# Four projections of a pair in one slot by halves of the array's rows, every second spell without a slot

## The chip, the cores and the metric

One core of a Trainium2 chip runs the whole program. The metric is the time of one execution in device microseconds; every comparison is between executions of two programs on the same chip.

## The reference

A transformer block on x of 4 x 1024 x 256 with a context of 4 x 64 x 192, all in float32, 16 heads of 64:

```python
h = _ln(x, g1, be1);  x = _attn(h, h, Wq1, Wk1, Wv1, Wo1, bo1) + x          # self-attention, 1024 keys
h = _ln(x, g2, be2);  x = _attn(h, context, Wq2, Wk2, Wv2, Wo2, bo2) + x    # cross-attention, 64 keys
h = _ln(x, g3, be3);  y = h @ Wp + bp                                       # 256 -> 2 x 1024
a, gate = y[..., :1024], y[..., 1024:]
x = a * gelu(gate) @ W2 + b2 + x
# _attn: q, k, v = projections to 16 heads of 64; softmax(q k^T / 8) v; @ Wo + bo
```

The change lies in the first line, the self-attention: each head's 1024 x 1024 scores, their softmax and the product with the values.

## The kernel before

**Spells.** Self-attention runs in NC = 64 spells. Spell C handles one pair of heads (pair P = C // 2, 32 pairs over four batches of x) and one half of the queries (c = C % 2, 512 of 1024). In what follows n = C % 16 is a spell's place in its batch. A spell on TensorE has three parts:

- eight rounds (one for each 128 keys): `score` (L464) makes the scores of both heads, three products of split operands each (L477) and one that subtracts the maxima (L481). The two heads use the array's upper and lower 64 rows, form `64*128`, and write different PSUM banks. Beside them `first_score` (L442) makes the unsplit scores of the next spell, from which VectorE takes the maxima (`row_max`, L777);
- `attend` (L484): the values' products, eight pairs of float32 matmuls on the left and right 64 columns of the array, form `128*64`. In even spells from C = 2 `sum_two` (L510, form `128*32`) stands ahead of them;
- a slot, `whole_array(slot(C))` (L533, L294), form `128*128`: `turn_max` (L457) turns the 128 x 128 tile of the next spell's maxima with one transpose, then come two `project_qk` (L418), each six matmuls of 512 columns. At c = 0 they make the second half of pair P + 1's queries and keys, at c = 1 the first half of pair P + 2's. Some slots also hold the turning of normalised rows for the next batch ("ln": n = 12 and 13, in the last batch 12 alone), four products with Wo of the batch before ("out1": n = 1 and 2 from the second batch on) or eight projections of values ("v": C % 8 = 7, but the last).

**Order.** Each engine's program is written out in one fixed order. TensorE's is the loop at L641 to L655. ScalarE: eight exponentials of 128 x 1024, copies of key sums, `write_oT` (L1103), then `split_qk` of the slot (L1076, its copy from PSUM). VectorE: 16 `row_max`, `gather_max` (L783), a reciprocal of the sums (L802), then the slot's jobs: `make_shift` (L790), `split_qk` (L769), and for "ln" `turn_half` (L730). GpSimd: seven additions of exponentials a spell, one scaling of an output, every second spell the splitting of a pair's weights.

**Banks.** There are eight PSUM banks: S0a, S0b, S1a, S1b take the rounds' scores in turn; T0 and T1 take head 0's first scores, PV and PJ head 1's, each bank every second round. The values' products go to S0a (in the last spell to PV). In a slot the maxima go to T1, the projections to S1b and PJ, "ln" to PV and T0. `bank_free` makes TensorE wait for the last reader of a bank.

Of the kernel before, what the change touches and what calls it, by code (L numbers as in the profile page):

```python
# [7 lines left out]
F32 = mybir.dt.float32  # L8
# [13 lines left out]
    ctx_turned ctx_product wq2_turned keys2_product values2_product ln_turned qk_projected v_projected first_scored0 first_scored1  # L22
# [26 lines left out]
def block_kernel(nc, x, ctx, Wq1, Wk1, Wv1, Wo1, bo1, Wq2, Wk2, Wv2, Wo2, bo2, Wp, bp, W2, b2,  # L49
# [33 lines left out]
    with stack:  # L83
# [115 lines left out]

        keys2_dram = nc.dram_tensor("keys2_all", (PART, B, KT * INNER), F32, kind="Internal").ap()  # L200
# [85 lines left out]
        def passed(C, t, half, head):  # L286

            return 2 * TILES * C + 2 * (CHUNKS * t + half) + head + 1
# [34 lines left out]
        def _(e):  # L323
# [93 lines left out]

            def project_qk(P, u, bank="PJ"):  # L418
                kind, c = (1 if u < 2 else 0), u % 2
                need.wait_ge(s.wqk_split, 2 * (P + 1))  # L420
                normed((1, P // PAIRS * CHUNKS + c))
                bank_free(bank)
                for i, (w, h) in enumerate(TERMS):
                    for k in range(KT):
                        last = e.matmul(banks[bank], wqk[:, P % 2, w, kind, k, :],  # L425
                                        hT[:, h, k, c * BANK:(c + 1) * BANK],
                                        start=(i == k == 0), stop=(i == 2 and k == KT - 1))
                last.then_inc(s.qk_projected, 1)
                free[bank] = ((s.split_lo, qk_of[P, u]),)
# [54 lines left out]
            def attend(R):  # L484
# [4 lines left out]
                bank = "S0a" if C + 1 < NC else "PV"  # L489
# [43 lines left out]
            def whole_array(jobs):  # L533
                for job in jobs:
                    if job[0] == "qk":
                        project_qk(*job[1:])
                    elif job[0] == "v":
                        project_v(*job[1:])
                    elif job[0] == "max":
                        turn_max(*job[1:])  # L540
                    elif job[0] == "out1":
                        out1(*job[1:])
                    else:
                        turn_half(*job[1:])

# [93 lines left out]
            project_qk(1, 0, "S1a")  # L639
            project_qk(1, 2, "S1b")  # L640
            for C in range(NC):  # L641
                for jt in range(TILES):
                    for part in range(len(TERMS) + 1):
                        for head in range(2):
                            score(TILES * C + jt, part, head)
                    if C + 1 < NC:
                        for head in range(2):
                            first_score(*next_part(C + 1, jt), head)
# [6 lines left out]
                whole_array(slot(C))  # L655
# [27 lines left out]
        def _(e):  # L683
# [85 lines left out]
            def split_qk(P, u, bank="PJ"):  # L769
# [4 lines left out]
                e.scalar_tensor_tensor(lo, banks[bank], SCALE if kind == 0 else 1.0, hi.bitcast(F32),  # L774
# [37 lines left out]
            def whole_array(jobs):  # L812
                for job in jobs:
# [4 lines left out]
                    elif job[0] == "max":  # L818
                        make_shift(*job[1:])
# [96 lines left out]
            split_qk(1, 0, "S1a")  # L916
            split_qk(1, 2, "S1b")
            for C in range(NC):
                b, n = divmod(C, BC)
                if C + 1 < NC:  # L920
                    for i in range(TILES):
                        for head in range(2):
# [63 lines left out]
        def _(e):  # L986
# [89 lines left out]
            def split_qk(P, u, bank="PJ"):  # L1076
# [4 lines left out]
                e.activation(qk[P % 2][:, 2 * kind, c * BANK:(c + 1) * BANK], banks[bank], ACT.Copy,  # L1081
# [21 lines left out]
            def write_oT(C):  # L1103
# [7 lines left out]
                e.copy(oT[:, P % PRING, c * BANK:(c + 1) * BANK], banks["S0a" if C + 1 < NC else "PV"]).then_inc(s.oT_written, 1)  # L1111
# [97 lines left out]
            split_qk(1, 0, "S1a")  # L1209
            split_qk(1, 2, "S1b")  # L1210
# [350 lines left out]
```

## Time and profile before

| | us |
|---|---|
| median of three executions (2042.30 to 2042.63) | 2042.55 |
| the profiled execution's own time | 2042.06 |
| its span | 2040.3 |
| TensorE matmuls busy | 2028.6 (99%) |
| GpSimd, VectorE, ScalarE busy | 1416.4, 1385.3, 1159.7 |
| granted clock of TensorE, mean | 1.00 |

The 64 spells run from 63.9 us to about 1512 us of the span. A matmul's recorded duration is longer than the time it takes from its neighbours, since matmuls are pipelined; the distance between starts is what a matmul costs. In the views a float32 matmul has two records, one of the split (float32r) operands one.

### The profile page before, as it was taken

Reading aid. Unit: us, or ns where it says so; the run is one execution under the profiler, and the core shown is the slowest. Engines: PE = TensorE matmul, PEld = TensorE weight load, DVE = VectorE, ACT = ScalarE, POOL = GpSimd, SP = SyncE. Lnnn points to the kernel's source line nnn. Section 1 sums busy time; section 2 is a strip of 40 time slices with the busy share of each in tenths; the row PEclk is TensorE's granted clock in tenths of the full one; section 3 lists DMA queues with packets and bytes.
Section 4 is the critical chain, followed back from the end, with each engine's and each line's share of the span. In section 5 each row is a group of like instructions: output and inputs, shape, how many; then the busy total and the mean of one; then the engine's idle time right before and its main releaser. Section 6 shows DMA issues by size and latency. Waiting matters only on the chain.

```text
span 2040.3 us, 31825 instructions
## 1 busy us (share of the span) xinstructions
PE 2028.6 (99%) x12500; PEld 1387.7 (68%) x12500; DVE 1385.3 (68%) x2124; ACT 1159.7 (57%) x1851; POOL 1416.4 (69%) x745
## 2 busy tenths in 40 slices
PE   8999999999999999999999999999999999999999
PEld 7665665666565566665655666566558999888888
DVE  6477677666767785578678566757777898754453
ACT  5566577544557675255667544657665666533332
POOL 2699799975979998679799867979895576300000
PEclk9999999999999999999999999999999999999999
DMA  7300000001000000010000001000010530000100
GB/s 229 124 7 21 6 7 16 6 6 47 17 11 6 16 6 6 1 63 6 6 6 22 6 1 52 6 6 1 22 47 16 145 84 1 1 21 22 42 11 31
DMA packets 46566, 58.74 MB, mean 29 GB/s; under 512 B 5969, under 2 KB 40401, under 8 KB 45265
## 3 DMA queue, kind: packets, MB, share of 16 engines
q1 hardware_dynamic: 46416, 56.71, 8.9%
q8 instruction: 98, 1.61, 0.3%
q14 instruction: 52, 0.42, 0.1%
HBM read 38.88 MB, written 17.83 MB: 28 GB/s over the span
## 4 chain that ended last, share of the span: by engine, by line
PE 99%; ACT 1%; DVE 0%; DMA 0%; issue 0%; SPq 0%; ACTq 0%
PE score L494 22%; PE score L477 18%; PE score L603 9%; PE score L481 6%; PE score L425 5%; PE attn_project L617 4%; PE attn_project L589 4%; PE score L559 4%; PE attn_project L425 4%; PE first_score L451 4%; PE attn_project L528 3%; PE score L437 3%; PE score L528 2%; PE attn_project L451 2%; PE first_score L518 2%; PE attn_project L437 1%
## 5 line engine op out<-in xcount | busy, mean ns | idle before, releaser
L1316 POOL TENSOR_TENSOR acc<-acc,pT 128x1024 f32<-128x1024 f32 x384 | 914.6, 2382 | 55.4 <-POOL acc L1316 0.9
L1100 ACT ACTIVATE pT<-score 128x1024 f32<-128x1024 f32 x512 | 525.7, 1027 | 102.8 <-PE score L481 59.1
L477 PE MATMUL score<-qk 64*128 64x512 f32 x3072 | 456.2, 399 | 1.5 <-ACT oT L1111 0.9
L494 PE MATMUL score<-pT,vT 128*64 128x512 f32 x2016 | 446.5, 595 | 0.0
L780 DVE TENSOR_REDUCE nmax<-first_score 128x1 f32<-128x512 f32 x512 | 347.9, 679 | 3.5 <-PE first_score L451 1.4
L780 DVE TENSOR_REDUCE nmax<-attn_project 128x1 f32<-128x512 f32 x512 | 347.1, 678 | 0.0
L477 PEld LDWEIGHTS score<-qk 64*128 64x128 f32 x3072 | 257.1, 184 | 120.7 <-ACT pT L1100 67.9
L494 PEld LDWEIGHTS score<-pT,vT 128*64 128x64 f32 x2016 | 139.1, 137 | 289.4 <-issue 251.8
L1313 POOL TENSOR_TENSOR acc<-pT 128x1024 f32<-128x1024 f32 x64 | 154.0, 2406 | 150.3 <-ACT pT L1100 150.3
L802 DVE RECIPROCAL sums<-sums 128x512 f32<-128x512 f32 (+1 forms) x65 | 214.4, 3299 | 57.5 <-ACT sums L1125 56.9
L481 PE MATMUL score<-shift,pick 64*128 64x512 f32 x1024 | 205.5, 391 | 0.0
L451 PE MATMUL first_score<-qk 64*128 64x512 f32 x512 | 200.8, 392 | 0.0
L451 PE MATMUL attn_project<-qk 64*128 64x512 f32 x512 | 200.6, 392 | 0.0
L603 PE MATMUL score<-hT,wp 128*128 128x512 f32 x768 | 183.9, 395 | 0.0
L1111 ACT COPY oT<-score 128x512 f32<-128x512 f32 x63 | 37.0, 588 | 229.8 <-PE score L494 229.8
L603 PEld LDWEIGHTS score<-hT,wp 128*128 128x128 f32 x768 | 142.4, 188 | 32.1
L1303 POOL TENSOR_TENSOR xres<-xres,rows 128x1024 f32<-128x1024 f32 x8 | 19.2, 2399 | 204.1 <-DVE xn L711 204.1
L774 DVE SCALAR_TENSOR_TENSOR qk<-score,qk 128x512 fp32r<-128x512 f32 x67 | 46.1, 690 | 151.7 <-ACT qk L1081 151.7
L1125 ACT COPY sums<-first_score 32x512 f32<-32x512 f32 x248 | 143.1, 577 | 9.1 <-PE first_score L518 6.2
L795 DVE TENSOR_TENSOR shift<-first_score,mask 128x512 fp32r<-128x512 f32 x64 | 44.2, 691 | 119.6 <-PE first_score L461 119.6
L1327 POOL TENSOR_TENSOR probs<-probs,rsum 128x1024 f32<-128x1024 f32 x32 | 61.0, 1907 | 91.5 <-DVE rsum L837 91.5
L1081 ACT ACTIVATE qk<-score 128x512 fp32r<-128x512 f32 x67 | 40.0, 598 | 143.6 <-PE score L425 143.6
(160 smaller groups left out, 3056.1 us busy)
## 6 DMA issues: line engine op xcount, KB each, us to landing
xres<-x_middle SPq DMA_DIRECT2D x10, 512.0 KB, 3.7
xres<-in_x SPq DMA_DIRECT2D x4, 1024.0 KB, 7.6
raw_qk<-in_L_xattn_Wq SPq DMA_DIRECT2D x32, 128.0 KB, 2.2
raw_qk<-in_L_xattn_Wk SPq DMA_DIRECT2D x32, 128.0 KB, 2.4
raw_v<-in_L_xattn_Wv SPq DMA_DIRECT2D x8, 512.0 KB, 4.1
keys_all<-keys SPq DMA_DIRECT2D x1, 4096.0 KB, 12.1
values_all<-values SPq DMA_DIRECT2D x1, 4096.0 KB, 12.4
out_x<-xres SPq DMA_DIRECT2D x7, 512.0 KB, 2.9
```

Source lines behind the costliest of these rows:

```text
L425: last = e.matmul(banks[bank], wqk[:, P % 2, w, kind, k, :], hT[:, h, k, c * BANK:(c + 1) * BANK], start=(i == k == 0), stop=(i == 2 and k ...
L451: last = e.matmul(banks[bank], qk[P % 2][r, w, q0:q0 + PART], qk[P % 2][r, 2 + h, half * BANK:(half + 1) * BANK], start=(m == 0), stop=(m ...
L477: e.matmul(bank, qk[P % 2][r, 2 + h, keys], qk[P % 2][r, w, queries], start=(part == 0), stop=False)
L481: e.matmul(bank, pick[r, :], shift[r, :], start=False, stop=True).then_inc(s.scored, 1)
L494: last = e.matmul(banks[bank][head * DH:(head + 1) * DH, :], vT[:, v_slot(D, jt), c0:c0 + DH], pT[:, jt, head, :], start=(jt == 0), stop=( ...
L603: last = e.matmul(banks[bank], wp[q][:, w, k, which, o:o + PART], hT[:, h, k, (c % 2) * BANK:(c % 2 + 1) * BANK], start=(term == k == 0), ...
L780: e.tensor_reduce(nmax[:, head, t, half:half + 1], banks[PASS_BANKS[head][half]], AX.X, ALU.max, negate=True).then_inc(s.row_max, 1)
L802: e.reciprocal(sums[:, C % 2, part], sums[:, C % 2, part]).then_inc(s.sum_inverse, len(halves))
L1100: e.activation(pT[:, jt].rearrange("p h n -> p (h n)"), SC[R % 2][:, :], ACT.Exp).then_inc(s.exponential, 1)
L1125: last = e.copy(sums[r * DH // 2:(r + 1) * DH // 2, o, :], banks[bank][g * DH // 2:(g + 1) * DH // 2, :])
L1313: e.tensor_tensor(total, pT[:, jt - 1], pT[:, jt], ALU.add).then_inc(s.probs_added, 1)
L1316: e.tensor_tensor(total, total, pT[:, jt], ALU.add).then_inc(s.probs_added, 1)
```

## The change

- `slot(C)` has no projections at c = 0; at c = 1 it makes all four of pair P + 2. 25 even spells (all but n = 12, and n = 2 from the second batch on) and C = 61 have nothing in the slot; there the values' products go to PV instead of S0a.
- Where such a c = 1 slot holds nothing else (17 spells: n = 3, 5, 9, 11 of each batch and n = 1 of the first), `project_qk_rows` does it by halves of the array's rows, form `64*128`: each `project_qk` of six matmuls of 512 columns over 128 rows becomes two turns of twelve matmuls of 256 columns over 64 rows. In a turn the upper rows work on one half of the 512 columns and the lower rows on the other, in two different banks; in the second turn they change over, and the halves add up in PSUM. Four such jobs go to the bank pairs FS (T0 and T1), PX (PV and PJ), S1 and FS again, in the order: first turns of jobs 1 and 2, second turns of 1 and 2, then the same for 3 and 4.
- In the other 13 c = 1 slots with projections all four are whole-array jobs as before, behind the slot's other work.
- `turn_max` is two float32 matmuls of 128 columns on the left and right 64 columns of the array, after the third pair of the values' products; `make_shift` moves ahead of VectorE's reciprocal.
- In the spell after a slot by rows, the first round has no first scores; those of its place are put around the second round's scores, head 1 ahead of head 0.
- Before the loop pair 1 gets all four projections instead of two.

```diff
+        HALF = BANK // 2
+        across = {"S1": SC[1][:, HALF:HALF + BANK], "PX": PX[:, HALF:HALF + BANK], "FS": FS[:, HALF:HALF + BANK]}
+        both = {"S1": ("S1a", "S1b"), "PX": ("PV", "PJ"), "FS": ("T0", "T1")}
...
         def slot(C):
-            jobs = [("max", C + 1, "T1")] if C + 1 < NC else []
...
-            jobs += [(*job, through[i % len(through)]) for i, job in enumerate(between)]
-            after = P + 1 + c
-            if after < B * PAIRS:
-                jobs += [("qk", after, 1 - c, "S1b"), ("qk", after, 3 - c, "PJ")]
+            jobs = [(*job, through[i % len(through)]) for i, job in enumerate(between)]
+            if c and P + 2 < B * PAIRS:
+                qk_banks = ("S1a" if "T0" in through else "T0", "T1", "S1b", "PJ") if between else ("FS", "PX", "S1", "FS")
+                jobs += [("qk", P + 2, u, bank) for u, bank in zip((0, 2, 1, 3), qk_banks)]
             return jobs
+        def by_rows(C):
+            return C >= 0 and any(job[-1] in both for job in slot(C))
+        def heads_of(C, n):
+            return (1, 0) if n == 0 and by_rows(C - 2) else (0, 1)
+        def value_bank(C):
+            return "S0a" if slot(C) else "PV"
...
+            def project_qk_rows(P, u, pair, turn):
+                kind, c = (1 if u < 2 else 0), u % 2
+                need.wait_ge(s.wqk_split, 2 * (P + 1))
+                normed((1, P // PAIRS * CHUNKS + c))
+                if turn:
+                    need.wait_ge(s.half_projected, half_of[P, u])
+                else:
+                    bank_free(*both[pair])
+                for i, (w, h) in enumerate(TERMS):
+                    for k in range(KT):
+                        for g in range(2):
+                            r, part = slice(g * DH, (g + 1) * DH), (g + turn) % 2 * HALF
+                            last = e.matmul(across[pair][:, part:part + HALF], wqk[r, P % 2, w, kind, k, :],
+                                            hT[r, h, k, c * BANK + part:c * BANK + part + HALF],
+                                            start=(i == k == turn == 0), stop=(i == 2 and k == KT - 1 and turn == 1))
+                            if i == 2 and k == KT - 1 and not turn:
+                                last.then_inc(s.half_projected, 1)
+                if turn:
+                    last.then_inc(s.qk_projected, 1)
+                    for bank in both[pair]:
+                        free[bank] = ((s.split_lo, qk_of[P, u]),)
...
             def turn_max(C, bank):
-                e.transpose(banks[bank][:, 0:PART], maxima[:, :], ident[:, :]).then_inc(s.max_turned, 1)
+                for head in range(2):
+                    m = slice(head * DH, (head + 1) * DH)
+                    last = e.matmul(banks[bank][m, 0:PART], maxima[:, m], ident[:, :], start=True, stop=True)
+                last.then_inc(s.max_turned, 1)
...
+            def rounds(C):
+                late = by_rows(C - 1) and C + 1 < NC
+                for jt in range(TILES):
+                    R = TILES * C + jt
+                    if late and jt == 1:
+                        first_score(*next_part(C + 1, 0), 1)
+                        for part in range(len(TERMS)):
+                            for head in range(2):
+                                score(R, part, head)
+                        first_score(*next_part(C + 1, 0), 0)
+                        for head in (1, 0):
+                            score(R, len(TERMS), head)
...
-            project_qk(1, 0, "S1a")
-            project_qk(1, 2, "S1b")
+            for u, bank in zip((0, 2, 1, 3), ("S1a", "S1b", "PV", "PJ")):
+                project_qk(1, u, bank)
             for C in range(NC):
...
                 for jt in range(TILES):
                     attend(TILES * C + jt)
-                whole_array(slot(C))
+                    if jt == 2 and C + 1 < NC:
+                        turn_max(C + 1, "T1")
+                slot_products(C)
...
@@ VectorE
-                        for head in range(2):
+                        for head in heads_of(C + 1, i):
                             row_max(*next_part(C + 1, i), head)
                     gather_max(C + 1)
+                    make_shift(C + 1, "T1")
```

## Rows read from the trace of the kernel before

**Rows 1.** The page: the chain by engine; a group (busy us, mean ns).
```profile
PE 99%; ACT 1%; DVE 0%; DMA 0%; issue 0%; SPq 0%; ACTq 0%
...
L494 PE MATMUL score<-pT,vT 128*64 128x512 f32 x2016 | 446.5, 595 | 0.0
```

**Rows 2.** Timeline of TensorE, C = 30 and 31 (start, duration, x records).
```profile
742.97 7.09 PE L494 MATMUL score<-pT,vT 128*64 128x512 f32 x32
749.98 0.33 PE L461 MATMUL first_score<-ident,maxima 128*128 128x128 f32 x1
750.07 1.64 PE L425 MATMUL score<-hT,wqk 128*128 128x512 f32 x6
751.55 1.56 PE L425 MATMUL attn_project<-hT,wqk 128*128 128x512 f32 x6
753.04 0.96 PE L477 MATMUL score<-qk 64*128 64x512 f32 x6
...
762.58 2.80 PE L494 MATMUL score<-pT,vT 128*64 128x512 f32 x12
```

**Rows 3.** Timeline, all engines, C = 61 to 62.
```profile
1473.62 2.74 PE L494 MATMUL score<-pT,vT 128*64 128x512 f32 x12
...
1477.05 0.96 PE L477 MATMUL score<-qk 64*128 64x512 f32 x6 [0.42 <-ACT oT L1111]
```

**Rows 4.** Timeline of TensorE in cross-attention: 256 columns, whole array, float32r.
```profile
1753.89 1.12 PE L589 MATMUL attn_project<-valuesB_lo,turned 128*128 128x256 f32 x8
1754.84 1.12 PE L589 MATMUL attn_project<-valuesB,turned_lo 128*128 128x256 f32 x8
```

**Rows 5.** Timeline of the weight loads in a round of C = 31.
```profile
757.36 0.18 PEld L451 LDWEIGHTS first_score<-qk 64*128 64x128 f32 x1
757.37 0.18 PEld L451 LDWEIGHTS attn_project<-qk 64*128 64x128 f32 x1
```

**Rows 6.** Timeline of ScalarE and VectorE, C = 30 and 31.
```profile
751.75 0.60 ACT L1081 ACTIVATE qk<-score 128x512 fp32r<-128x512 f32 x1 [1.06 <-PE score L425]
752.38 0.69 DVE L774 SCALAR_TENSOR_TENSOR qk<-score,qk 128x512 fp32r<-128x512 f32 x1 [1.34 <-ACT qk L1081]
...
754.51 0.69 DVE L780 TENSOR_REDUCE nmax<-first_score 128x1 f32<-128x512 f32 x1
...
764.20 0.17 DVE L787 TENSOR_REDUCE maxima<-nmax 128x8 f32<-128x16 f32 x1
764.28 3.35 DVE L802 RECIPROCAL sums<-sums 128x512 f32<-128x512 f32 x1
```

**Rows 7.** Timeline, all engines, the slot of C = 28 (n = 12).
```profile
707.57 0.33 PE L461 MATMUL first_score<-ident,maxima 128*128 128x128 f32 x1
707.74 0.60 PE L337 MATMUL attn_project<-ident,xn 128*128 128x128 f32 x4
708.17 0.60 PE L337 MATMUL first_score<-ident,xn 128*128 128x128 f32 x4
...
711.50 0.69 DVE L741 TENSOR_TENSOR hT<-first_score,hT 128x512 fp32r<-128x512 f32 x1
...
712.53 0.39 PE L451 MATMUL first_score<-qk 64*128 64x512 f32 x1
```

**Rows 8.** Timeline, all engines, the slot of C = 29 (n = 13).
```profile
728.21 0.33 PE L461 MATMUL first_score<-ident,maxima 128*128 128x128 f32 x1
...
732.17 0.69 DVE L741 TENSOR_TENSOR hT<-first_score,hT 128x512 fp32r<-128x512 f32 x1
```

**Rows 9.** Timeline of GpSimd, C = 30 and 31.
```profile
737.72 0.65 POOL L1267 TENSOR_SCALAR wqk<-raw_qk 128x512 fp32r<-128x512 f32 x1
738.45 1.30 POOL L1269 TENSOR_TENSOR wqk<-raw_qk,wqk 128x512 fp32r<-128x512 f32 x1
...
760.30 1.29 POOL L1322 TENSOR_TENSOR oT<-oT,sums 128x512 f32<-128x512 f32 x1
...
764.08 12.47 POOL L1316 TENSOR_TENSOR acc<-acc,pT 128x1024 f32<-128x1024 f32 x5
```

More of the change, by code:

```diff
@@ L198, in block_kernel, with place @@
                  "S1b": SC[1][:, BANK:], "T0": FS[:, 0:BANK], "T1": FS[:, BANK:], "PV": PX[:, 0:BANK], "PJ": PX[:, BANK:]}
+        HALF = BANK // 2
+        across = {"S1": SC[1][:, HALF:HALF + BANK], "PX": PX[:, HALF:HALF + BANK], "FS": FS[:, HALF:HALF + BANK]}
+        both = {"S1": ("S1a", "S1b"), "PX": ("PV", "PJ"), "FS": ("T0", "T1")}
+        def place(bank):
+            return across[bank] if bank in both else banks[bank]
         keys2_dram = nc.dram_tensor("keys2_all", (PART, B, KT * INNER), F32, kind="Internal").ap()
@@ L308, in slot @@
             through = ("PV", "T0") if between and between[0][0] == "ln" else ("PV", "S0b", "S1a")
-            jobs += [(*job, through[i % len(through)]) for i, job in enumerate(between)]
-            after = P + 1 + c
-            if after < B * PAIRS:
-                jobs += [("qk", after, 1 - c, "S1b"), ("qk", after, 3 - c, "PJ")]
-            return jobs
+            jobs = [(*job, through[i % len(through)]) for i, job in enumerate(between)]
+            if c and P + 2 < B * PAIRS:
+                qk_banks = ("S1a" if "T0" in through else "T0", "T1", "S1b", "PJ") if between else ("FS", "PX", "S1", "FS")
+                jobs += [("qk", P + 2, u, bank) for u, bank in zip((0, 2, 1, 3), qk_banks)]
+            return jobs
+        def by_rows(C):
[4 more added lines that the diff above has]
+            return "S0a" if slot(C) else "PV"
+        half_of = {job[1:3]: 2 * (i + 1) for i, job in enumerate(
+            job for C in range(NC) for job in slot(C) if job[-1] in both)}
         def last_out1(i):
@@ L488, in attend @@
                 need.wait_ge(s.exponential, R + 1)
-                bank = "S0a" if C + 1 < NC else "PV"
+                bank = value_bank(C)
                 if jt == 0:
@@ L531, in out1, with slot_products @@
                 free[bank] = ((s.x1_added, TILES * b + t + 1),)
-            def whole_array(jobs):
-                for job in jobs:
+            def slot_products(C):
+                if by_rows(C):
+                    jobs = slot(C)
+                    for two in (jobs[0:2], jobs[2:4]):
+                        for turn in range(2):
+                            for job in two:
+                                project_qk_rows(*job[1:], turn)
+                    return
+                for job in slot(C):
                     if job[0] == "qk":
@@ L544, in whole_array @@
                         turn_half(*job[1:])
+            def rounds(C):
[10 more added lines that the diff above has]
+                            score(R, len(TERMS), head)
+                    else:
+                        for part in range(len(TERMS) + 1):
+                            for head in range(2):
+                                score(R, part, head)
+                    if C + 1 < NC and not (late and jt == 0):
+                        for head in range(2):
+                            first_score(*next_part(C + 1, jt), head)
             def score2(i):
@@ L638, in _ @@
             turn_max(0, "T1")
-            project_qk(1, 0, "S1a")
-            project_qk(1, 2, "S1b")
+            for u, bank in zip((0, 2, 1, 3), ("S1a", "S1b", "PV", "PJ")):
+                project_qk(1, u, bank)
             for C in range(NC):
-                for jt in range(TILES):
-                    for part in range(len(TERMS) + 1):
-                        for head in range(2):
[L645 to L648, printed above, removed]
+                rounds(C)
                 if C == NC - 1:
@@ L915, in _ @@
             make_shift(0, "T1")
-            split_qk(1, 0, "S1a")
-            split_qk(1, 2, "S1b")
+            for u, bank in zip((0, 2, 1, 3), ("S1a", "S1b", "PV", "PJ")):
+                split_qk(1, u, bank)
             for C in range(NC):
@@ L1080, in split_qk @@
                     need.wait_ge(s.scored, 4 * TILES * (P - 1))
-                e.activation(qk[P % 2][:, 2 * kind, c * BANK:(c + 1) * BANK], banks[bank], ACT.Copy,
+                e.activation(qk[P % 2][:, 2 * kind, c * BANK:(c + 1) * BANK], place(bank), ACT.Copy,
                              scale=SCALE if kind == 0 else 1.0).then_inc(s.split_hi, 1)
@@ L1110, in write_oT @@
                     need.wait_ge(s.out1_product, TILES * b + TPC * (c + 1))
-                e.copy(oT[:, P % PRING, c * BANK:(c + 1) * BANK], banks["S0a" if C + 1 < NC else "PV"]).then_inc(s.oT_written, 1)
+                e.copy(oT[:, P % PRING, c * BANK:(c + 1) * BANK], banks[value_bank(C)]).then_inc(s.oT_written, 1)
             def copy_sums(C, bank="PJ"):
@@ L1208, in _ @@
                     fetch_table(ACT.Exp, 1)
-            split_qk(1, 0, "S1a")
-            split_qk(1, 2, "S1b")
+            for u, bank in zip((0, 2, 1, 3), ("S1a", "S1b", "PV", "PJ")):
+                split_qk(1, u, bank)
             for C in range(NC):
```

12 lines of the change are left out of this document (4 added, 8 removed).

## The prediction

> **What bounds the kernel now.** The page first: TensorE is busy for 99% of the span, the granted clock is 1.00 of full speed (2.4 GHz) throughout, and the chain that ended last is 99% TensorE [rows 1]. The other engines are busy for 57% to 69%. So in the 64 spells only two things change the time: work added to or taken from TensorE's queue, and waits of TensorE that were not there. Then TensorE's timeline by spell, which is very regular. An odd spell (C = 31) starts its rounds at 753.04 and its values' products at 762.58, 9.54 us; eight pairs of values' products take 7.0 us (742.97 to 749.98, the way out included); then one transpose, twelve projection matmuls and back to scores at 753.04 [rows 2]. Even spells have 1.0 us more for the sums.
>
> **Prices on TensorE.** I take distances between starts, and where a merged row hides the last start, its end less one recorded duration.
> - Values' products: 12 records in 2.74 us, the last one's 0.59 [rows 1] off, leaves 2.15 us for five steps of two records, 0.43 each [rows 3]. So a record of 512 float32 columns costs 0.43 us, two column halves at once; a pair of matmuls is two such steps.
> - Way from them to the whole array: they end at 742.97 + 7.09 = 750.06, the last starts 0.59 earlier, at 749.47; the transpose starts at 749.98, 0.51 later, against 0.43 in the stream: 0.09 [rows 2]. The transpose itself costs 0.09 (749.98 to 750.07).
> - Projections: 12 matmuls from 750.07 to 753.04, 2.97 us. Six start in 1.48 (to 751.55), the other six take 1.49 with the way out. The last six have ended at 751.55 + 1.56 = 753.11 by record, each 0.40 long, so their last starts at 752.71, and their five steps are 0.232 each. From there to the scores it is 0.33, 0.10 over a step; the first six took 0.08 over six steps. Together a visit to `128*128` costs 0.18 us beside its work.
> - Projection of 256 columns: whole-array float32r matmuls of that width run eight in 0.95 (1753.89 to 1754.84), 0.12 each [rows 4]. By rows two run side by side: the 40 pairs of 512 columns in a spell's rounds take 9.54 us with the changes of form in it [rows 2], 0.24 at most, as much as one whole-array matmul of that width, and the two weight loads of a pair start 10 ns apart, 757.36 and 757.37 [rows 5]. So I take 0.12 a pair.
>
> **Part by part**, as additions to the total. The number of projections stays 128, so their matmul time cancels except where the form changes.
>
> (1) *The turning of the maxima.* Now two float32 matmuls of 128 columns beside each other: two steps of a quarter of 0.43, 0.215 us, in place of a transpose of 0.09, 63 times: +13.5 - 5.5 = +8. From below it can't be under the two quarter steps, as nothing beside it leaves TensorE idle; from above a full 0.43. I take the quarter: columns set the step. Its wait: the maxima are gathered at 764.20 + 0.17 = 764.37 [rows 6], 1.8 us behind the start of the values' products at 762.58; the third pair ends 2.6 us behind it. Margin 0.8 us, in even spells 1.8; the other five pairs of values' products stand behind this wait, and after them the slot.
>
> (2) *Visits to the whole array.* Without one are now the 25 even spells, the 17 by rows and C = 61: 43 visits. 41 times 0.18 = -7.4. The slots of C = 61 and 62 held the transpose alone, and 1.28 us lay between the last values' product and the scores; of that 0.42 was a wait for ScalarE's copy out of S0a [rows 3]. A direct way is 0.51, so these two save 0.75 each less the transpose counted in (1), -1.3; in C = 61 the values' products now wait for the maxima of PV, about +0.6. Sum -8.1.
>
> (3) *By rows.* 48 pairs of 0.12 are 5.76 us against 24 of 0.2325, 5.58: +0.18, 17 times: +3. Bounds: from below 0.107 a pair, a quarter of the step of 0.43 as in (1), which gives -7.5 instead of +3 in all; the upper one stands under rival B.
>
> (4) *The bank pair FS, used twice in a slot.* Job 4 may start when VectorE has read job 1. A turn is six pairs, and the first pair after a change of form costs 0.1 more: job 1 ends behind 18 pairs, at 2.26 us of the slot, and job 4 could start behind 30, at 3.70. The last matmul of a job is over 0.16 behind its step (1.12 less seven steps of 0.12 is a duration of 0.28 [rows 4]); 0.04 later the copy starts (751.55 + 0.16 against 751.75), VectorE 0.63 after it, for 0.69 [rows 2, 6]. 2.26 + 0.16 + 0.04 + 0.63 + 0.69 and 0.04 back to TensorE are 3.82; the restart costs 0.1 again: +0.22, 17 times: +3.7. Bounds 0 and 0.6. The copy is not late: the exponentials ended long before, and VectorE's reciprocal of 3.35 us, now behind `make_shift`, ends about 6.9 us after the start of the values' products (2.6 + 0.2 for the maxima, 0.1, 0.69, 3.3); the slot starts at 7.1. The waits of a second turn for its first have the other job's turn, 0.72, as cover. Behind the slot the last job's operands are split 1.47 us after the scores start, as now (754.51 against 753.04); the first score in T0 comes at 1.8, which is what the changed order is for. Nothing there.
>
> (5) *n = 12, "ln" alone, four times.* The transposes into T0 end, and the next round's first score wants T0. Today 2.8 us of projections lie between, and T0 is free at 711.50 + 0.69 = 712.19, before the first score at 712.53 [rows 7]. Now the turning starts at 707.57, ends near 708.65, rounds start there, and the first score would come at 709.7. ScalarE's copy of the values and its pass over PV come first as today, so VectorE's four steps behind them move 0.1 at most: T0 is free at 712.1. Wait 2.4, restart 0.1: +2.5 each, +10. The 2.8 us of projections leave this slot, and nearly all of it comes back as a wait. Bounds 0 and 2.8.
>
> (6) *n = 13, "ln" and four projections, three times.* The third projection (u = 1) reads the rows that the same slot has just turned. They are split at 732.17 + 0.69 = 732.86 [rows 8]. The turning starts at 728.21, eight transposes of 0.11 (four from 707.74 to 708.17 [rows 7]), two projections of 1.4: 732.0. Wait 0.9 each: +2.8. Before, only the halves of the rows that were ready were projected there.
>
> (7) *Start and the rest.* Two changes of form for `turn_max(0)`, +0.5; in C = 0 the values' products wait for PV, +0.35. Slots with "out1" and "v" keep their work. GpSimd: seven additions of 12.47/5 = 2.49 are 17.5 us, a scaling 1.3, every second spell 2.0 of weights [rows 9]: 39.6 us for two spells, against about 40.6 of TensorE's. The short spells (17.8) let it fall about 3 us behind, the long ones (22.8) give it back; an exponential waits for the addition one spell back, at least 6 us away. Nothing.
>
> Sum: +8.0 - 8.1 + 3.0 + 3.7 + 10.0 + 2.8 + 0.9 = +20.3. By this the profiled execution of 2042.06 becomes 2062.4; the median of the runs lies 0.5 above that execution, so I predict 2063 us, 1.0% slower.
>
> One rule would move (3). The Trainium skill, TensorEngine Tiling (Array Packing), Instruction Overhead, gives each matmul about 60 cycles on top. At full clock, by that page, a pair of 256 columns would be an estimated 0.13 instead of 0.12, and the sum about 8 us higher. The trace disagrees: its 0.12 a matmul at this width [rows 4] holds whatever comes on top.
>
> **Rivals.**
>
> *A, the waits are covered.* If (4) to (6) come to nothing, +3.8 is left: 2046.3. For it: TensorE waits for almost nothing now. Against: (5) is arithmetic from four VectorE steps in a row.
>
> *B, two loads and two matmuls in 0.12 us are too many.* A pair by rows is four instructions; the densest row here is a load and a matmul in 0.11 us, four transposes from 707.74 to 708.17 [rows 7]. If that is a limit on instructions, or if the loads of both row halves share it, a pair costs 0.22: 48 x 0.10 = 4.8 us a slot, 82 in 17 slots: 2145. Against it: the two loads 10 ns apart [rows 5]. A partial case (0.13 to 0.16 a pair) adds 8 to 33. The Trainium skill, TensorE: Matmul & The Clock Gate, LDWEIGHTS, has a load last by its columns and not its rows, so halving the rows saves nothing: an estimated 0.107 us each, and if two went one after another, 0.21 a pair.
>
> *C, faster: a change of form costs more than I read.* In C = 61 and 62 the slot took 1.28 us for one transpose [rows 3]. If everything beyond a bare step of 0.43 is the visit and its drain, it is worth 0.85, not the 0.27 of visit and transpose, at all 43 places: 25 us more saved, 2038. It decides from 0.75 a visit. Against it: half of that 1.28 is named as a wait for a copy, and in ordinary slots the starts leave only 0.18.
>
> *D, the half-long spells put GpSimd on the path.* Margin 1.0 us in 40; if it is used up, some 1 to 2 us in each of 17: 2080.
>
> **How the numbers follow.** Forecast 0.72, A 0.08, B with its partial cases 0.10, C 0.06, D 0.04. The forecast's own range is 2054 to 2074: (5) and (6) may halve, (4) double, a pair be 0.115 to 0.13. For 8 in 10 with something of A, D and the mild part of B: 2048 to 2082. Within 0.2% (4.1 us) can't be told from no change: faster 0.07 (C), same 0.06 (half of A, a little of C), slower 0.87.
>
> **What would show it.** Starts of the values' products: third to fourth pair 1.07 apart instead of 0.86. A slot without work: 0.5 us from the last values' product to the scores. A slot by rows: 6.6 us, steps of 0.12 a pair, one stop of 0.2 ahead of job 4. At n = 12 an idle TensorE of 2.4 us ahead of a first score, released by VectorE's hT; at n = 13 one of 0.9 ahead of a projection. Wrong if a pair's step isn't near 0.12, if the two "ln" slots show no idle time, or if the maxima's matmuls wait for VectorE.

## The result, and the profile after

| | before | after |
|---|---|---|
| median, us (4 executions each, same chip) | 2042.59 (2042.30 to 2042.66) | 2066.70 (2066.26 to 2067.17) |
| ratio, 95% interval | | 1.0118 (1.0101 to 1.0136) |
| profiled execution, us | 2042.06 | 2067.17 |
| its span, us | 2040.3 | 2065.4 |

The kernel became 1.2% slower: 24 us by the medians, 25.1 by the spans. Forecast was 2063, with 2048 to 2082 as the range.

The page of the kernel after, busy time by engine and the chain by engine, to be read against [rows 1]:

```profile
PE 2041.1 (99%) x13916; PEld 1431.0 (69%) x13916; DVE 1385.3 (67%) x2124; ACT 1159.6 (56%) x1851; POOL 1416.2 (69%) x745
...
PE 95%; DVE 2%; ACT 1%; DMA 1%; issue 0%; POOL 0%; SPq 0%; DVEq 0%; ACTq 0%
```

TensorE bounds it as before, but VectorE now holds 2% of the chain that was 99% TensorE. The waits of TensorE (waited for: us in total, times, longest) say where. For these three lines the kernel before has no counterpart at these places:

```profile
PE first_score L500 <- DVE hT L817: 9.7, 4, 2.4
...
PE score L474 <- DVE hT L817: 2.4, 3, 0.8
...
PE attn_project L547 <- DVE nmax L856: 0.7, 2, 0.4
```

They sum to 12.8 us, half of the loss. Two waits for ScalarE at C = 61 and 62, 0.9 us in all before (one is in [rows 3]), are gone. The other half is work and clock. I lined up the 64 spells of both traces by the starts of their first rounds' score, first values' product and last values' product. Change after minus before, us:

| part of a spell | places | each |
|---|---|---|
| ahead of the first spell (12 projections more, 2.79) | 1 | +2.98 |
| values' products | 63 | +0.22 |
| slot, now empty (12 projections gone), without C = 62 | 24 | -3.05 |
| slot by rows (12 projections more) | 17 | +3.00 |
| slot with "v" or "out1" (12 more) | 10 | +2.74 |
| slot with "out1", n = 2 (12 fewer) | 3 | -2.86 |
| slot n = 12 (12 fewer) | 4 | -2.90 |
| rounds behind it | 4 | +2.52, twice 1.5 on top |
| slot n = 13 (12 more) | 3 | +3.72 |
| rounds n = 14 | 3 | -0.29 |
| slot C = 61, 62 (only the transpose before, empty now) | 2 | -0.76 |
| wait for PV ahead of the values' products, C = 0 and 61 | 2 | +0.12, +0.43 |

All other rounds stay within 0.05. The last spell starts 24.05 us later than before.

**The turning.** TensorE's timeline of the kernel after, C = 2 (start, duration, records, [idle before]):

```profile
117.47 2.80 PE L547 MATMUL attn_project<-pT,vT 128*64 128x512 f32 x12
120.10 0.39 PE L513 MATMUL first_score<-ident,maxima 128*64 128x128 f32 x4
120.32 4.46 PE L547 MATMUL attn_project<-pT,vT 128*64 128x512 f32 x20
124.71 0.96 PE L530 MATMUL score<-qk 64*128 64x512 f32 x6
```

From 120.10 to 120.32 are the 0.22 us of the two turning matmuls, with no idle time before them. Then the twenty records end at 124.78, their last starts at 124.19, and the scores start at 124.71: 0.52 without a slot.

**A slot by rows.** Timeline of the kernel after, C = 1, all engines:

```profile
100.90 0.99 PE L457 MATMUL first_score<-hT,wqk 64*128 64x256 f32 x12
101.72 0.87 PE L457 MATMUL attn_project<-hT,wqk 64*128 64x256 f32 x12
102.43 0.87 PE L457 MATMUL first_score<-hT,wqk 64*128 64x256 f32 x12
103.14 0.87 PE L457 MATMUL attn_project<-hT,wqk 64*128 64x256 f32 x12
103.35 0.60 ACT L1156 ACTIVATE qk<-first_score 128x512 fp32r<-128x512 f32 x1 [1.74 <-PE first_score L457]
103.85 0.87 PE L457 MATMUL score<-hT,wqk 64*128 64x256 f32 x12
103.98 0.69 DVE L850 SCALAR_TENSOR_TENSOR qk<-first_score,qk 128x512 fp32r<-128x512 f32 x1 [6.56 <-ACT qk L1156]
104.72 0.97 PE L457 MATMUL first_score<-hT,wqk 64*128 64x256 f32 x12
105.53 0.87 PE L457 MATMUL score<-hT,wqk 64*128 64x256 f32 x12
...
106.95 0.86 PE L530 MATMUL score<-qk 64*128 64x512 f32 x6
```

A turn of six pairs takes 0.71 us (101.72 to 102.43). The first takes 0.82. The fifth, ahead of job 4, takes 0.87, since job 4 waits for VectorE to have read `first_score`: 103.98 + 0.69 = 104.67, and job 4 starts at 104.72. Its restart makes the sixth turn 0.81. From the start of the last values' product to the scores the slot took 6.57 us.

**n = 12.** Timeline of the kernel after, C = 28 to 29:

```profile
720.40 0.60 PE L362 MATMUL first_score<-ident,xn 128*128 128x128 f32 x4
720.93 0.96 PE L530 MATMUL score<-qk 64*128 64x512 f32 x6
721.42 0.82 DVE L812 TENSOR_SCALAR attn_project<-attn_project,cols 128x512 f32<-128x512 f32 x1 [1.73 <-ACT hT L1116]
722.27 0.69 DVE L817 TENSOR_TENSOR hT<-attn_project,hT 128x512 fp32r<-128x512 f32 x1
722.88 0.81 DVE L812 TENSOR_SCALAR first_score<-first_score,cols 128x512 f32<-128x512 f32 x1
723.72 0.69 DVE L817 TENSOR_TENSOR hT<-first_score,hT 128x512 fp32r<-128x512 f32 x1
724.56 0.47 PE L500 MATMUL first_score<-qk 64*128 64x512 f32 x1 [2.44 <-DVE hT L817]
```

VectorE's four steps fill 721.42 to 724.41, and the first score in T0 stands behind the last of them, where before 2.8 us of projections ran [rows 7].

**The clock.** Windows of the kernel after behind the four waits of n = 12, C = 13, 29, 45 and 61 (length, busy time and records of each engine, granted clock, DMA share, GB/s), each from the end of the wait or up to one microsecond behind it:

```profile
343.90:347.40 3.50, 3.50 (x20) 3.27 (x19) 2.56 (x4) 1.02 (x1) 3.36 (x3) 0.51 0.02 5
...
724.60:728.10 3.50, 3.50 (x30) 3.17 (x32) 3.03 (x6) 1.94 (x2) 3.36 (x2) 1.00 0.00 0
1105.10:1108.60 3.50, 3.50 (x21) 3.16 (x19) 2.34 (x5) 1.58 (x2) 3.36 (x3) 0.51 0.01 2
1485.40:1488.90 3.50, 3.50 (x30) 3.04 (x32) 3.02 (x6) 1.92 (x2) 0.95 (x1) 1.00 0.00 0
```

Behind two of the four, TensorE runs at half speed (0.51, the level of 1.2 GHz), with 20 records in 3.5 us where 30 pass at 1.00. Their rounds took 4.05 and 4.08 us more instead of 2.52. That is 3.1 us in all, and I had no term for it.

### The profile page after: what moved, and what is told of

It is laid out like the page before. It is cut to its first block, busy times and chain, and to the rows that moved or that the text cites. A ratio compares the mean times of both kernels' runs of the same rounds, so it can differ in the third digit from the quotient of the medians.

```text
span 2065.4 us, 34701 instructions
## 1 busy us (share of the span) xinstructions
PE 2041.1 (99%) x13916; PEld 1431.0 (69%) x13916; DVE 1385.3 (67%) x2124; ACT 1159.6 (56%) x1851; POOL 1416.2 (69%) x745
## 4 chain that ended last, share of the span: by engine, by line
PE 95%; DVE 2%; ACT 1%; DMA 1%; issue 0%; POOL 0%; SPq 0%; DVEq 0%; ACTq 0%
PE score L530 17%; PE score L547 13%; PE attn_project L547 9%; PE score L683 9%; PE score L534 6%; PE attn_project L697 4%; PE first_score L500 4%; PE score L639 4%; PE attn_project L669 4%; PE attn_project L581 3%; PE score L486 3%; PE first_score L457 3%; PE score L581 2%; PE first_score L571 2%; PE attn_project L486 1%; PE first_score L474 1%
## 5 line engine op out<-in xcount | busy, mean ns | idle before, releaser
L530 PEld LDWEIGHTS score<-qk 64*128 64x128 f32 x3072 | 262.0, 185 | 119.2 <-ACT pT L1175 64.3
L547 PE MATMUL score<-pT,vT 128*64 128x512 f32 x1184 | 268.5, 595 | 0.0
L547 PE MATMUL attn_project<-pT,vT 128*64 128x512 f32 x864 | 195.7, 595 | 0.7 <-DVE nmax L856 0.7
L547 PEld LDWEIGHTS score<-pT,vT 128*64 128x64 f32 x1184 | 80.4, 137 | 143.5 <-issue 126.8
L850 DVE SCALAR_TENSOR_TENSOR qk<-first_score,qk 128x512 fp32r<-128x512 f32 x57 | 39.4, 691 | 159.5 <-ACT qk L1156 159.2
L547 PEld LDWEIGHTS attn_project<-pT,vT 128*64 128x64 f32 x864 | 58.8, 137 | 115.4 <-issue 93.7
```

The costliest lines, as they stand in the source:

```text
L530: e.matmul(bank, qk[P % 2][r, 2 + h, keys], qk[P % 2][r, w, queries], start=(part == 0), stop=False)
L547: last = e.matmul(banks[bank][head * DH:(head + 1) * DH, :], vT[:, v_slot(D, jt), c0:c0 + DH], pT[:, jt, head, :], start=(jt == 0), stop=( ...
```

## Experiments

The theory: turning the maxima in float32, the two "ln" slots and the form by rows each cost what their places in the table above show. The rivals: the cost comes from the other parts, and would stay if one of these is undone. The kernel before was run again beside the experiments, with a median of 2042.89 us beside the first four (`turn_only` to `four_banks`) and of 2042.50 beside the last four; each ratio is to the median beside it. Differences to `after` are taken across these measurements, and `before` lay within 0.4 us in all of them.

**turn_only**: the kernel before, with the new turning alone.

```diff
-            jobs = [("max", C + 1, "T1")] if C + 1 < NC else []
+            jobs = []
...
-                e.transpose(banks[bank][:, 0:PART], maxima[:, :], ident[:, :]).then_inc(s.max_turned, 1)
+                for head in range(2):
+                    m = slice(head * DH, (head + 1) * DH)
+                    last = e.matmul(banks[bank][m, 0:PART], maxima[:, m], ident[:, :], start=True, stop=True)
+                last.then_inc(s.max_turned, 1)
...
                     attend(TILES * C + jt)
+                    if jt == 2 and C + 1 < NC:
+                        turn_max(C + 1, "T1")
...
                     gather_max(C + 1)
+                    make_shift(C + 1, "T1")
```

> The kernel before, with one part of the change alone: the maxima are turned by two float32 matmuls of 128 columns among the values' products, behind the third pair, and the shift is made then. Slots and projections as before. My theory: two steps of 0.107 us for a transpose of 0.09, 63 times, +8 us, so 2051; the values' products last 0.22 longer in every spell and TensorE waits for nothing new. Rival, the wait: if the maxima come later than the third pair, TensorE stands there for VectorE and it costs more than 10. Rival, hidden: no difference from 2042.6.

Measured: 2052.33 (2051.88 to 2053.73), ratio 1.0048 (1.0035 to 1.0062), span 2050.5: 9.4 us more than before by the medians, 10.2 by the spans. Timeline of TensorE in this kernel:

```profile
767.64 2.80 PE L497 MATMUL score<-pT,vT 128*64 128x512 f32 x12
770.26 0.39 PE L463 MATMUL first_score<-ident,maxima 128*64 128x128 f32 x4
770.48 4.46 PE L497 MATMUL score<-pT,vT 128*64 128x512 f32 x20
```

The same 0.22 in each of 63 spells. The transpose that left the slot gave back 0.05 to 0.07, 0.10 to 0.11 in the "ln" slots and nothing at C = 61 and 62; the rounds didn't move. The last spell starts 10.35 us later, 10.0 of it from the spells and 0.3 from the start. So this part alone is 40% of the loss, and a transpose in the stream of whole-array matmuls was cheaper than its 0.09 in the trace looked.

**ln_covered**: the kernel after, with the projections around "ln" as before (two at n = 11, two at n = 12), so that n = 12 has its 2.8 us of cover back and n = 13 keeps its four.

```diff
-            if c and P + 2 < B * PAIRS:
+            if n in (BC - 5, BC - 4):
+                jobs += [("qk", P + 1 + c, 1 - c, "S1b"), ("qk", P + 1 + c, 3 - c, "PJ")]
+            elif c and P + 2 < B * PAIRS:
```

> The changed kernel, with the two spells n = 11 and n = 12 as before the change: two whole-array projections in each slot, so that two of them stand behind the turning of the rows at n = 12 again. Theory: the four waits for T0 (2.4 us each) go, the pair of spells (11, 12) gets 2.8 us shorter in each batch, -11; and the two stretches of half clock right behind two of these waits go with them, 1.5 us each, -3: 2052.5, granted clock 1.00 throughout. Rival: the half clock has another cause and stays: 2055.5. Rival: the wait only moves to another bank or to a later spell: 2064 or more.

Measured: 2053.71 (2052.72 to 2053.81), ratio 1.0052 (1.0040 to 1.0065), span 2051.9: 13 us less than after. Of TensorE's waits `first_score <- DVE hT` is gone and the one of n = 13 is left. The waits, and TensorE's timeline at C = 28 to 29:

```profile
PE score L476 <- DVE hT L819: 2.4, 3, 0.8
```
```profile
717.91 0.96 PE L532 MATMUL score<-qk 64*128 64x512 f32 x6
718.95 0.39 PE L502 MATMUL first_score<-qk 64*128 64x512 f32 x1
```

The first score follows the scores without idle time, and the granted clock is 1.00 in the windows where it had been 0.51. The wait at n = 12 and the clock behind it are worth 10.1 + 3.1; the experiment gives 13.0 by the medians, 13.5 by the spans. Its edit does more than take the wait away: the n = 11 slots lose their form by rows with the stop, and slots n = 11 and 12 together are 0.26 shorter, 1.0 us in all. The first spell starts 1.5 us later than in `after`, with nothing edited ahead of it. So the sum isn't exact to a microsecond. The wait and the half clock go at once; that the clock falls because of the wait rests on this and on its place, in every trace, at such a wait.

**turn_one_pass**: the kernel after, with the maxima and the identity in bfloat16, so that each turning matmul is one record. The maxima that are subtracted are thereby rounded to bfloat16.

```diff
-            ("maxima", [PART], F32),
+            ("maxima", [2 * PART], BF16),
...
-                    last = e.matmul(banks[bank][m, 0:PART], maxima[:, m], ident[:, :], start=True, stop=True)
+                    last = e.matmul(banks[bank][m, 0:PART], maxima[:, m], ident_h[:, :], start=True, stop=True)
...
+            e.tensor_scalar(ident_h[:, :], ident[:, :], 1.0, 1.0, ALU.mult, ALU.mult).then_inc(s.const, 1)
```

> The changed kernel, with the maxima and the identity in bfloat16 for the turning, so that the two matmuls of 128 columns are one record each instead of two float32 records. The shift of a row is rounded, the same for the whole row. Theory: columns set the price, so a quarter of the float32 price: 0.055 instead of 0.215 us a spell, -10 us, 2056.6. Rival: a matmul that short has a floor of its own, such as the transpose's 0.09 to 0.11: -7, 2060. Rival: what the turning costs is the two entries and their loads, not the columns: no change, 2066.7.

Measured: 2059.60 (2059.02 to 2059.67), ratio 1.0082 (1.0068 to 1.0096), span 2057.8. By the medians it gives 7.1, between the two expectations, and needs both traces to be read. Timeline of TensorE, C = 2:

```profile
117.96 2.80 PE L549 MATMUL attn_project<-pT,vT 128*64 128x512 f32 x12
120.59 0.23 PE L515 MATMUL first_score<-ident_h,maxima 128*64 128x128 bf16 x2
120.64 3.60 PE L549 MATMUL attn_project<-pT,vT 128*64 128x512 f32 x16
```

The turning takes 0.05 to 0.06 now, so all of the 0.16 a spell came, 10.1 us, and the rival's floor of 0.09 to 0.11 isn't there. But half clock stood behind all four "ln" waits in this profile, not two. Its windows at C = 13 and 61:

```profile
342.00:346.00 4.00, 3.98 (x21) 3.66 (x23) 2.50 (x4) 1.02 (x1) 3.86 (x2) 0.57 0.00 0
...
1479.00:1483.00 4.00, 4.00 (x25) 3.77 (x24) 2.90 (x6) 2.05 (x2) 2.38 (x1) 0.59 0.00 0
```

Two more times 1.5 us take 3 of the 10 back.

**four_banks**: the kernel after, with a bank pair for each job of a slot by rows, so that no job waits for VectorE; the first scores of the next spell go head 0 first, as FS is read first.

```diff
-        across = {"S1": SC[1][:, HALF:HALF + BANK], "PX": PX[:, HALF:HALF + BANK], "FS": FS[:, HALF:HALF + BANK]}
-        both = {"S1": ("S1a", "S1b"), "PX": ("PV", "PJ"), "FS": ("T0", "T1")}
+        across = {"S0": SC[0][:, HALF:HALF + BANK], "S1": SC[1][:, HALF:HALF + BANK], "PX": PX[:, HALF:HALF + BANK], "FS": FS[:, HALF:HALF + BANK]}
+        both = {"S0": ("S0a", "S0b"), "S1": ("S1a", "S1b"), "PX": ("PV", "PJ"), "FS": ("T0", "T1")}
...
-                qk_banks = ("S1a" if "T0" in through else "T0", "T1", "S1b", "PJ") if between else ("FS", "PX", "S1", "FS")
+                qk_banks = ("S1a" if "T0" in through else "T0", "T1", "S1b", "PJ") if between else ("FS", "S0", "S1", "PX")
...
-            return (1, 0) if n == 0 and by_rows(C - 2) else (0, 1)
+            return 0, 1
...
+                        first_score(*next_part(C + 1, 0), 0)
+                        for part in range(len(TERMS)):
+                            for head in (1, 0):
+                                score(R, part, head)
                         first_score(*next_part(C + 1, 0), 1)
-                        for part in range(len(TERMS)):
-                            for head in range(2):
-                                score(R, part, head)
-                        first_score(*next_part(C + 1, 0), 0)
-                        for head in (1, 0):
+                        for head in (0, 1):
                             score(R, len(TERMS), head)
```

> The changed kernel, with four different bank pairs for the four jobs of a slot by rows (FS, S0, S1, PX instead of FS, PX, S1, FS), and with head 0's first score ahead of head 1's in the second round behind it, as PX is now the last to come free. Theory: the stop ahead of job 4 (0.16 us, and 0.11 for the restart) goes in 17 slots, -4.6, 2062.1. Rival: the wait moves: job 2 stands for the copy out of S0a, or the next rounds for PX, and nothing is won.

Measured: 2062.36 (2061.46 to 2064.97), ratio 1.0098 (1.0085 to 1.0112); the profiled execution is the slowest of the four. The slot by rows took 0.22 less than after's, 17 times: 3.8 us; the stop is gone. Of the medians' 4.3, then, the slots explain the most, and the execution with after's mean clock of 0.998 (2063.05) lies 3.65 under after's median. The clock fell at two waits again (C = 29 and 45), and at C = 29 for longer: from 721.65, while TensorE still waited (the wait ends at 722.31), to 728.48. Windows at C = 29, the first from 0.3 us ahead of the end of the wait, the second over the return of the clock:

```profile
722.00:725.00 3.00, 2.69 (x12) 2.33 (x14) 1.45 (x3) 0.15 (x1) 2.86 (x2) 0.50 0.00 0
725.60:732.30 6.70, 6.70 (x50) 5.30 (x46) 5.40 (x10) 4.38 (x5) 6.56 (x4) 0.79 0.01 2
```

**four_whole**: the kernel after, with the 17 slots by rows as whole-array projections in four banks.

```diff
-                qk_banks = ("S1a" if "T0" in through else "T0", "T1", "S1b", "PJ") if between else ("FS", "PX", "S1", "FS")
+                qk_banks = ("S1a" if "T0" in through else "T0", "T1", "S1b", "PJ")
```

> The changed kernel, with the four projections of the 17 slots by rows as whole-array jobs again (banks T0, T1, S1b, PJ) and the usual order of the first scores; every second spell stays without a slot. It says what the form by rows is worth. Theory by the rows of the changed kernel: a slot by rows is 6.56 us, a whole-array one 3.51 + 12 x 0.2325 = 6.30; so 0.24 less in 17 slots, -4, 2062.6. Rival, the change's own idea: leaving the array's form alone is worth more than halving costs, so this is slower, by 0.2 to 0.5 a slot: 2070 to 2075.

Measured: 2061.27 (2059.35 to 2064.54), ratio 1.0088 (1.0074 to 1.0102). Timeline of TensorE, C = 1:

```profile
101.73 3.07 PE L474 MATMUL first_score<-hT,wqk 128*128 128x512 f32 x12
104.64 1.56 PE L474 MATMUL score<-hT,wqk 128*128 128x512 f32 x6
106.04 1.56 PE L474 MATMUL attn_project<-hT,wqk 128*128 128x512 f32 x6
107.53 0.73 PE L530 MATMUL score<-qk 64*128 64x512 f32 x4
```

The slot is 0.25 shorter than by rows with the stop, 4.3 us in 17, and as long within 0.03 as by rows with four bank pairs (+2.75 and +2.78 on the kernel before). The medians give 5.4, because three of the five executions here had a mean clock of 1.00 and all of `after` 0.998. So the form by halves of the rows wins nothing over the whole array even without its stop: what it saves on the change of form it spends on turns of 0.71 against 0.70 for three whole-array matmuls and on its own first pairs.

**plain_order**: the kernel after, without the changed order of the first scores behind a slot by rows.

```diff
-                late = by_rows(C - 1) and C + 1 < NC
+                late = False
...
-            return (1, 0) if n == 0 and by_rows(C - 2) else (0, 1)
+            return 0, 1
```

> The changed kernel, with the first round behind a slot by rows as in every spell: the first scores of both heads behind the first round's scores. Theory: T0 is read until 1.53 us behind the start of the rounds, the first score wants it at 0.92, so TensorE waits 0.6 and restarts for 0.1, 17 times: +12, 2078, with DVE qk as the releaser. Rival: the other head's order covers nothing, no change: 2066.7.

Measured: 2079.06 (2078.53 to 2080.31), ratio 1.0179 (1.0165 to 1.0193). Waits of TensorE, and its timeline at C = 2:

```profile
PE first_score L500 <- DVE qk L850: 10.0, 17, 0.6
```
```profile
108.97 0.46 PE L500 MATMUL first_score<-qk 64*128 64x512 f32 x1 [0.59 <-DVE qk L850]
```

Each of the 17 rounds behind a slot by rows is 0.7 longer. The order is worth 12 us, and it is why I could put nothing there in the forecast.

**turn_only_one_pass**: `turn_only` with bfloat16 maxima, and **all_mended**: the kernel after with bfloat16 maxima, four bank pairs, and two projections a slot from n = 11 to 14. In both the subtracted maxima are rounded as above. Their edits are those shown for `turn_only`, `turn_one_pass` and `four_banks`, and in `all_mended` this one:

```diff
-            if c and P + 2 < B * PAIRS:
+            if n in range(BC - 5, BC - 1):
+                if P + 1 + c < B * PAIRS:
+                    jobs += [("qk", P + 1 + c, 1 - c, "S1b"), ("qk", P + 1 + c, 3 - c, "PJ")]
+            elif c and P + 2 < B * PAIRS:
```

> The kernel before, with the maxima turned among the values' products as in the run turn_only, and in bfloat16 as in turn_one_pass. Theory: the turning then costs 0.06 us, as much as the transpose that it takes the place of (leaving it out of the slot gave 0.06): 2042.6 to 2043. If this is clearly faster than the kernel before, the transpose had a price in the slot that the starts don't show.

> The changed kernel with what the runs so far found: bfloat16 maxima (-10.1), four bank pairs in the 13 slots by rows that are left (-2.9), two projections a slot at n = 11 to 14, so that two stand behind each turning of rows (-11 and -3 of half clock at n = 12, -1.6 at n = 13 and 14). From 2066.7: 2038 to 2039.5, that is 3 to 4.5 us less than the kernel before. Theory: the gains add, since each is TensorE's own time or a wait of its own. Rival: once these waits are gone the short spells put another engine on the path, GpSimd first, and TensorE waits for additions of exponentials: 2045 or more.

Measured: `turn_only_one_pass` 2043.11 (2041.88 to 2043.76), ratio 1.0002 (0.9993 to 1.0011), no change; `all_mended` 2038.53 (2037.11 to 2039.62), ratio 0.9979 (0.9971 to 0.9988), a small gain of 0.2% with the interval clear of 1. Its one new wait of TensorE in the spells, and its slot by rows at C = 1 (0.82 for the first turn, then 0.70 to 0.76, no stop):

```profile
PE attn_project L552 <- DVE nmax L861: 0.9, 2, 0.6
```
```profile
100.52 0.98 PE L462 MATMUL first_score<-hT,wqk 64*128 64x256 f32 x12
101.34 0.91 PE L462 MATMUL score<-hT,wqk 64*128 64x256 f32 x12
102.10 0.87 PE L462 MATMUL first_score<-hT,wqk 64*128 64x256 f32 x12
102.80 1.59 PE L462 MATMUL score<-hT,wqk 64*128 64x256 f32 x24
```

The two differ in what the slots hold, with what follows from it: four projections ahead of the loop, PV for the products of spells with an empty slot, and the order of the first scores behind a slot by rows. So having no slot in every second spell is worth 2043.1 - 2038.5 = 4.6 us, 0.2%, or 5.0 by the starts of the last spell (the two profiled spans differ by 3.0, as 2 us more lie behind the spells in `all_mended`, see below). Spells n = 11 to 14 have no part in it, as their slots are as before, but for C = 61 and 62, which are empty in `all_mended`. That is the prize of the idea once its three prices are gone. By the last spell's start `all_mended` is 4.8 us ahead of the kernel before.

## Why the prediction was right

The forecast lay 4 us under the result, in its own range, and most of its terms came near their size. By its steps, as terms of the span (predicted, then measured by the spells):

| step | predicted | measured |
|---|---|---|
| (1) turning | +8.0 | +10.0 (`turn_only`, without the start) |
| (2) visits | -8.1 | about -7.7 |
| (3) by rows | +3.0 | +1.7 |
| (4) FS twice | +3.7 | +4.4 |
| (5) n = 12 | +10.0 | +10.1 |
| (6) n = 13 | +2.8 | +3.1 |
| (7) start, PV in C = 0 | +0.9 | +0.3 |
| half clock | none | +3.1 |
| rounds n = 14 | none | -0.9 |
| behind the spells | none | +1.1 |

These come to 25.2 against 25.1; the 0.02 to 0.05 by which rounds differ either way are the rest. Of the 4.8 us between 20.3 and 25.1, the clock is 3.1 and the turning 2.0; the smaller misses nearly cancel.

(1) The two quarter steps were right, 0.22 against 0.215. What failed is the other half of the term, the transpose taken out at 0.09: it gave 0.055 in an ordinary slot, and nothing at C = 61 and 62. I had read a start-to-start distance right behind a change of form, where the first matmul's own distance isn't its price.

(2) Right in sum by two errors. 24 empty slots saved 0.26 each beside their projections; with `turn_only`'s 0.055 for the transpose, 0.205 of it is the visit, against 0.18: -4.9. But a slot by rows isn't free of a visit: its first turn has 0.11 on top and saves only 0.1 (-1.7 for 17). C = 61 and 62 gave -1.5, and the wait of C = 61's values' products cost 0.43 against 0.6.

(3) A turn takes 0.71, so the eight take 5.68 us against 5.58 on the whole array: +0.10 a slot, where 0.12 a pair gave +0.18. Rival B falls with it: the chip runs two loads and two matmuls in 0.12 us. TensorEngine Tiling (Array Packing), Instruction Overhead, of the Trainium skill would have put a pair at an estimated 0.13; six pairs in 0.71 us disagree.

(4) The stop is 0.16 and the restart 0.10, 0.26 against 0.22, and `four_banks` took out 0.22. Job 4 was ready at 3.82 us of the slot in my working and starts at 3.82 behind job 1 (104.72 less 100.90).

(5) The wait was to be 2.4 and is 2.42 to 2.44, with 0.08 to 0.1 of restart. Of the 2.8 us of projections that left the slot 2.4 came back as idle time, as the working said. (6) was to be 0.9 and is 0.8, with a slot 0.1 longer beside it. Rival A, that these waits are covered, falls with the waits themselves, and `ln_covered` shows that two projections would have covered the one at n = 12. At n = 14 the rounds had 0.29 us more than other even spells in the kernel before, and the change took that away; I did not see it. In `all_mended`, whose slot n = 13 is as before, the 0.29 is back (10.82 against 10.55), so it goes with that slot; why is open.

(7) The start is +0.2 beside its 12 projections (2.98 less 2.79) where 0.5 was forecast, and C = 0 waits 0.12 for PV instead of 0.35. The start isn't known closely: in the six experiments on the changed kernel the first spell starts 2.9 to 4.5 us later than before, with nothing edited there. GpSimd holds 0% of the chain and isn't in the waits of the spells, so rival D is out. Rival C needed 0.75 a visit; the runs show 0.2.

**The missed term** is the clock. Working (5) said 2.4 us of idle TensorE, four times, and stopped there; the profile before showed a clock of 1.00 in a kernel where TensorE never idled so long in the spells, which is no evidence for one where it does ([rows 1], which the prediction names for it, holds no clock). Beside `after`, the same waits of 2.4 us had half clock behind all four (`turn_one_pass`), two (`four_banks`, `plain_order`) and one of them (`four_whole`). With the two of `after`, that is 11 of 20 waits. It differs between executions of one program too: the mean clock of the five executions of `four_whole` was 0.998, 1.00, 1.00, 0.998 and 1.00, at 2064.54, 2059.35, 2059.46, 2062.53 and 2061.27 us, while all four of `after` had 0.998. The range covered the term by luck of its width, not by a reason.

The last us behind the spells is likewise no part of the change: over the eight experiments' profiles the stretch behind the last spell's start differs from the kernel before by -0.1 to +1.9 us, `all_mended`'s most of all. Nothing there was edited. The four profiles with 1.1 us or more (`after`, `four_whole`, `plain_order`, `all_mended`) have one or two waits of TensorE for GpSimd or VectorE in cross-attention that the kernel before lacks, 0.5 to 0.7 us each. Why they come in these profiles is open.

## What to carry to other kernels

Moving work out of a stage in which another engine still has to finish isn't a saving: add up that engine's chain first, as the 2.8 us at n = 12 shows, and allow for half clock at part of the new waits, as at 11 of 20 here. Small operations in a form that needs no change still cost their columns in their own type: float32 turning cost more in 63 spells than the visits saved, and bfloat16 turning a quarter of it. When an idea comes with several edits, price each at its number of places; here the idea was worth 4.6 us (`turn_only_one_pass` less `all_mended`), and its details had cost 28 (`after` less `all_mended`).

## What the runs showed of the hardware

- Half clock after an idle TensorE of only 2.4 us: for about 3.4 us (in `after` from 343.97 to 347.39, the wait ending at 343.39) at a price of 1.5 us. Twice in 11 it lasted 6.8 us, and both times it had set in some 0.6 us before the wait was over (`four_banks` at C = 29, `four_whole` at C = 61). Windows of `four_whole` at the last of these waits, which ends at 1479.37, then once it is over:

```profile
1478.70:1485.50 6.80, 6.13 (x29) 5.24 (x31) 4.16 (x7) 2.05 (x2) 2.86 (x2) 0.50 0.00 0
1486.00:1489.00 3.00, 3.00 (x28) 2.34 (x26) 2.81 (x5) 2.70 (x3) 2.86 (x2) 1.00 0.03 8
```

  There the price was 2.7 us (rounds +5.69, where the wait for PV and the 2.52 make 2.95), and 2.8 in `four_banks`. At 9 other waits of the same 2.4 us the clock stayed at 1.00. What decides between them wasn't settled.
- Two float32r matmuls of 256 columns on the two halves of the rows, in different banks, take 0.12 us together with their two loads (0.71 for six pairs), no more than one on the whole array [rows 4].
- Two matmuls of 128 columns beside each other take 0.22 us in float32 (two records each) and 0.06 in bfloat16 (one record each), between values' products of the same form. That is about a quarter, where half the records would give half; why wasn't looked into. Nor was turning in float32r on half the columns.
